# Gated attention block on one core: a batch's routing scratch moved into its PSUM bank, small normalisation steps moved or folded

## The reference

```python
x = x + tanh(g_xattn) * xattn(layernorm(x), ctx)      # windows of 128 columns, 8 heads of 32
x = x + tanh(g_ffn)   * ffn(layernorm(x))             # layernorm over the last axis, eps = 1e-5

def ffn(hidden):                                      # row of 2048 values per (batch, d)
    logits = flat @ router_weight.T + router_bias     # 64 experts
    scores = softmax(logits)
    topk_w, topk_idx = top_k(scores, 8)
    w_dense = scatter(topk_w, topk_idx)
    return flat * topk_w.sum() + w_dense @ expert_bias
```

## Time and profile before

| | us |
|---|---|
| median of 3 runs | 1213.76 |
| lowest, highest | 1210.02, 1215.45 |
| the profiled execution, its own time | 1211.18 |
| its span, first to last instruction | 1209.0 |
| mean granted clock of TensorE, share of full speed | 0.987 |

### The profile page before, as it was taken

How to read it: one execution, slowest core, us unless ns; L and a number is a source line. 1 busy time by engine, 2 the same in 40 slices (tenths; PEclk the granted TensorE clock), 3 DMA queues, 4 the chain that set the end, 5 groups by cost and what they waited for, 6 DMA issues and landing times.

```text
span 1209.0 us, 33323 instructions
## 1 busy us (share of the span) xinstructions
PE 1125.2 (93%) x11661; PEld 1045.5 (86%) x11661; DVE 975.0 (81%) x1882; ACT 1028.9 (85%) x3200; POOL 707.7 (59%) x660
## 2 busy tenths in 40 slices
PE   3699999999999899999999999998999999999977
PEld 3698999889988899798997989988998889979955
DVE  6667878988789877989779977988779987797757
ACT  4688999889989899988998989898898889989944
POOL 2365777467655567557764666646764656655621
PEclk9899999999999999999999999999999999999989
DMA  9267554785548854596546865478444884555433
GB/s 289 75 175 198 139 131 116 232 214 149 132 116 249 222 130 126 147 261 181 128 127 216 217 165 129 115 244 226 117 126 123 259 218 120 130 161 178 104 85 139
DMA packets 169766, 199.82 MB, mean 165 GB/s; under 512 B 27776, under 2 KB 104704, under 8 KB 169472
## 3 DMA queue, kind: packets, MB, share of 16 engines
q1 hardware_dynamic: 168736, 197.69, 60.3%
q10 hardware_dynamic: 864, 0.01, 0.0%
HBM read 80.06 MB, written 33.65 MB: 94 GB/s over the span
## 4 chain that ended last, share of the span: by engine, by line
PE 53%; SPq 21%; DVE 9%; ACT 5%; issue 5%; DMA 4%; POOL 3%; DVEq 0%; ACTq 0%; POOLq 0%
SPq L520 14%; PE ring L309 7%; PE ring L311 6%; PE ring L310 6%; PE ring L365 4%; DVE X L888 3%; PE ring L348 3%; PE ring L324 3%; PE ring L326 3%; PE ring L325 3%; PE ring L384 3%; PE ring L385 3%; PE ring L386 3%; SPq L525 3%; PE ring L403 3%
## 5 line engine op out<-in xcount | busy, mean ns | idle before, releaser
L614 ACT ACTIVATE P<-ring,nmx 128x128 f32<-128x128 f32 x1024 | 358.6, 403 | 32.1 <-DVE nmx L754 31.8
L309 PE MATMUL ring<-z_hi,wqk_hi 128*128 128x256 f32 x1024 | 299.3, 292 | 22.9 <-DVE z_lo L953 21.0
L310 PE MATMUL ring<-z_hi,wqk_lo 128*128 128x256 f32 x1024 | 292.3, 285 | 0.0
L311 PE MATMUL ring<-z_lo,wqk_hi 128*128 128x256 f32 x1024 | 292.2, 285 | 0.0
L614 ACT ACTIVATION_READ_ACCUMULATOR P<-ring,nmx 128x1 f32 x1024 | 248.9, 243 | 0.0
L1046 POOL TENSOR_TENSOR z_lo<-z,z_hi 128x1024 fp32r<-128x1024 f32 x62 | 147.6, 2381 | 166.8 <-ACT z_hi L582 166.8
L309 PEld LDWEIGHTS ring<-z_hi,wqk_hi 128*128 128x128 f32 x1024 | 198.0, 193 | 35.4 <-DVE wqk_lo L928 20.9
L1058 POOL TENSOR_TENSOR X<-X,xt 128x512 f32<-128x512 f32 x128 | 165.5, 1293 | 68.3 <-DVE xt L789 68.2
L761 DVE STREAM_TRANSPOSE T<-P 128x512 f32<-128x512 f32 x256 | 169.1, 690 | 44.6 <-ACT P L614 28.2
L311 PEld LDWEIGHTS ring<-z_lo,wqk_hi 128*128 128x128 f32 x1024 | 198.7, 194 | 0.0
L310 PEld LDWEIGHTS ring<-z_hi,wqk_lo 128*128 128x128 f32 x1024 | 198.5, 194 | 0.0
(11 more groups left out here) (137 smaller groups left out, 2696.1 us busy)
## 6 DMA issues: line engine op xcount, KB each, us to landing
PT<-T SPq DMA_DIRECT2D x1024, 80.0 KB, 2.1
cx<-in_ctx SPq DMA_DIRECT2D x128, 256.0 KB, 3.7
out_y<-X SPq DMA_DIRECT2D x128, 256.0 KB, 3.1
X<-in_x SPq DMA_DIRECT2D x112, 256.0 KB, 4.7
mg<-in_mask SPq DMA_DIRECT2D x64, 128.0 KB, 3.3
X<-in_x SPq DMA_DIRECT2D x8, 512.0 KB, 7.5
sel<-rows_d SPq DMA_DIRECT2D x256, 3.0 KB
X<-in_eb SPq DMA_DIRECT2D x2, 512.0 KB, 8.2
```

Source lines behind the costliest of these rows:

```text
L309: e.matmul(o, wqk_hi[:, t, cols], z_hi[:, t, :], t == 0, False)
L310: e.matmul(o, wqk_lo[:, t, cols], z_hi[:, t, :], False, False)
L311: last = e.matmul(o, wqk_hi[:, t, cols], z_lo[:, t, :], False, t == DT - 1)
L614: last = e.activation(P[:, n, :], bank("S", 4 * u + g)[:, k * W:(k + 1) * W], ACT.Exp, bias=nmx[u % 2][:, n:n + 1], accum_out=den[u % 2][: ...
```

## The change

- `lr` is gone. Its content is written into the unused half of the logits' own PSUM bank (`low(b)`); the product with the exponentials goes there too, and so do the sum of the weights and the gain in `c_scale`. That bank is now given back when `c_scale` is done (semaphore `ac_v`), at slot 40.75, and no longer at `c_top`'s (`lg_v`, slot 38.75).
- `c_gate` and `gate` are gone. `c_scale` makes the gain with one scalar_tensor_tensor and the bias with another, from `mv2` and `rs2`.
- The negated means are gone: the first normalisation subtracts the mean (`mv` is in two buffers for it), the second puts -1 in its formula.
- The eps additions leave VectorE; GpSimd adds eps, waits for itself, and raises to the power.

```diff
-            for b in batch(t, C["LT"]):
-                take(("LT", b), t, C["c_top"] - C["LT"], lg_v, b + 1)
+                take(("LT", b), t, C["c_sc"] - C["LT"], ac_v, b + 1)
...
             def norm2(b):                                  # VectorE
                 e.wait_ge(bn2_v, 16 * (b + 1))
+                if b:
+                    e.wait_ge(ac_v, b)
                 for t in range(DT):
                     e.bn_aggr(mv2[:, t, :], bn2[:, t, :, :].rearrange("p a c -> p (a c)")).then_inc(agg2_v, 1)
-                if b:
-                    e.wait_ge(ac_v, b)
-                e.wait_ge(agg2_v, DT * (b + 1))
-                e.tensor_scalar(ln2[:, 0, :], mv2[:, :, 0], -1.0, None, ALU.mult).then_inc(neg2_v, 1)
-                e.tensor_scalar(ln2[:, 1, :], mv2[:, :, 1], EPS, None, ALU.add).then_inc(neg2_v, 1)
...
-                e.wait_ge(rstd2_g, b + 1)
-                e.tensor_scalar(gate[:, 0, :], ln2[:, 2, :], cst[:, TF:TF + 1], None, ALU.mult).then_inc(dm_v, 1)
-                e.wait_ge(dm_v, b + 1)
-                e.tensor_tensor(gate[:, 1, :], gate[:, 0, :], ln2[:, 0, :], ALU.mult).then_inc(gate_v, 1)
...
-                    last = e.match_replace(lr[:, t, :], t8[:, t, :], lg[:, t, :], -3.0e38)
+                    last = e.match_replace(low(b)[:, t, :], t8[:, t, :], lg[:, t, :], -3.0e38)
                 last.then_inc(mr_v, 1)
                 e.wait_ge(mr_v, b + 1)
-                e.tensor_tensor(lr[:], lr[:], lg[:], ALU.not_equal).then_inc(sel_v, 1)
+                e.tensor_tensor(low(b), low(b), lg[:], ALU.not_equal).then_inc(sel_v, 1)
+
+            def low(b):
+                return bank("LT", b)[:, DT * NX:2 * DT * NX].rearrange("p (t x) -> p t x", t=DT)
...
-                e.tensor_tensor(ex[:], ex[:], lr[:], ALU.mult).then_inc(wm_v, 1)
+                e.tensor_tensor(low(b), low(b), ex[:], ALU.mult).then_inc(wm_v, 1)
...
-                e.tensor_reduce(sc[:, :, 5:6], w2[:, :, 0, :], AX.X, ALU.add).then_inc(wm_v, 1)
-                e.wait_ge(gate_v, b + 1)
+                wsum, gain = bank("LT", b)[:, 0:DT], bank("LT", b)[:, DT:2 * DT]
+                e.tensor_reduce(wsum, w2[:, :, 0, :], AX.X, ALU.add).then_inc(wm_v, 1)
                 e.wait_ge(wm_v, 4 * b + 3)
-                e.tensor_tensor(sc[:, :, 4:5], sc[:, :, 5:6], gate[:, 0, :].unsqueeze(2), ALU.mult).then_inc(wm_v, 1)
-                e.tensor_tensor(sc[:, :, 7:8], sc[:, :, 5:6], gate[:, 1, :].unsqueeze(2), ALU.mult)
+                e.scalar_tensor_tensor(out=gain, in0=wsum, scalar=cst[:, TF:TF + 1], in1=rs2[:], op0=ALU.mult,
+                                       op1=ALU.mult).then_inc(wm_v, 1)
                 e.wait_ge(wm_v, 4 * b + 4)
-                e.tensor_scalar(sc[:, :, 6:7], sc[:, :, 4:5], 1.0, None, ALU.add).then_inc(ac_v, 1)
+                e.scalar_tensor_tensor(out=sc[:, :, 7], in0=gain, scalar=-1.0, in1=mv2[:, :, 0], op0=ALU.mult, op1=ALU.mult)
+                e.tensor_scalar(sc[:, :, 6], gain, 1.0, None, ALU.add).then_inc(ac_v, 1)
...
             def norm2(b):                                  # GpSimd; input_norm in the same way
-                e.wait_ge(neg2_v, 2 * (b + 1))
-                e.tensor_tensor(ln2[:, 2, :], ln2[:, 1, :], half[:], ALU.pow).then_inc(rstd2_g, 1)
+                e.wait_ge(agg2_v, DT * (b + 1))
+                e.tensor_scalar(rs2[:], mv2[:, :, 1], EPS, None, ALU.add).then_inc(eps2_g, 1)
+                e.wait_ge(eps2_g, b + 1)
+                e.tensor_tensor(rs2[:], rs2[:], half[:], ALU.pow).then_inc(rstd2_g, 1)
```

More of the change, by code:

```diff
@@ L52 @@
     hT=37.5, hT_gap=0.25, ht_hi=41.25, ht_lo=41.75, R=47.25,
-    norm2=27.5, c_gate=33.5, L=36, LT=34, c_top=38.75, c_exp=37.75, c_w=40.75, c_sc=40.75, wT=43, wt_hi=43.25, wt_lo=42.25, mix=43.75, m_gap=0.25,
+    norm2=27.5, L=36, LT=34, c_top=38.75, c_exp=37.75, c_w=40.75, c_sc=40.75, wT=43, wt_hi=43.25, wt_lo=42.25, mix=43.75, m_gap=0.25,
     sx=44.75, sx_gap=1.25, x2=45.25, rl=48.5, rl_gap=2,
@@ L139, in gated_block_kernel @@
         bnst = sb("bnst", [128, DT, 4, 6])
-        mv = sb("mv", [128, DT, 2])
+        mv = [sb(f"mv{i}", [128, DT, 2]) for i in range(2)]
         bn2 = sb("bn2", [128, DT, 4, 6])
         mv2 = sb("mv2", [128, DT, 2])
-        ln1 = [sb(f"ln1_{i}", [128, 3, DT]) for i in range(2)]
-        ln2 = sb("ln2", [128, 3, DT])
+        rs1 = [sb(f"rs1_{i}", [128, DT]) for i in range(2)]
+        rs2 = sb("rs2", [128, DT])
         L = sb("L", [128, D])
@@ L195, in gated_block_kernel @@
         out_done = [[sem(f"out{t}{c}") for c in range(4)] for t in range(DT)]
-        bn1_v, agg1_v, neg1_v, rstd1_g = (sem(n) for n in ("bn1", "agg1", "neg1", "rstd1"))
+        bn1_v, agg1_v, eps1_g, rstd1_g = (sem(n) for n in ("bn1", "agg1", "eps1", "rstd1"))
         st_a = sem("st")
@@ L202, in gated_block_kernel @@
         gelu_a, othi_a, otlo_g, wo_pe, xt_v, x1_g = (sem(n) for n in ("gelu", "othi", "otlo", "WO", "xt", "x1"))
[L203 to L206, removed]
+        bn2_v, agg2_v, eps2_g, rstd2_g, ht_pe, hthi_a, htlo_v, r_pe = (sem(n) for n in (
+            "bn2", "agg2", "eps2", "rstd2", "hT", "hthi", "htlo", "R"))
+        l_a, lt_pe, lg_v, t8_v, neg_v, mr_v, sel_v, ex_a, w2_v, ac_v = (sem(n) for n in (
+            "L", "LT", "lg", "t8", "neg", "mr", "sel", "ex", "w2", "ac"))
         wm_v, wT_pe, wthi_a, wtlo_v, mix_pe, sx_a, x2_v = (sem(n) for n in (
@@ L835, in c_top @@
                     last = e.scalar_tensor_tensor(out=lg[:, t, :], in0=bank("LT", b)[:, t * NX:(t + 1) * NX],
-                                                  scalar=ln2[:, 2, t:t + 1], in1=rbb[:], op0=ALU.mult, op1=ALU.add)
+                                                  scalar=rs2[:, t:t + 1], in1=rbb[:], op0=ALU.mult, op1=ALU.add)
                 last.then_inc(lg_v, 1)
@@ L941, in _ @@
             input_norm(0)
-            ln = ln1[0]
             e.wait_ge(rstd1_g, 1)
@@ L945, in _ @@
                 for t in range(h.start, h.stop):
-                    last = e.tensor_scalar(z32[:, t, :], X[0][:, t, 0:U], ln[:, 0, t:t + 1], ln[:, 2, t:t + 1],
-                                           ALU.add, ALU.mult)
+                    last = e.tensor_scalar(z32[:, t, :], X[0][:, t, 0:U], mv[0][:, t, 0:1], rs1[0][:, t:t + 1],
+                                           ALU.subtract, ALU.mult)
                 last.then_inc(z32_g, 1)
@@ L1008, in _ @@
                         r_low(u, a)
-                for b in batch(t, C["c_gate"]):
-                    c_gate(b)
                 for b in batch(t, C["c_top"]):
@@ L1038, in z_full @@
                 for t in range(DT):
-                    last = e.tensor_scalar(z32[:, t, :], X[b % 2][:, t, c * U:(c + 1) * U], ln[:, 0, t:t + 1],
-                                           ln[:, 2, t:t + 1], ALU.add, ALU.mult)
+                    last = e.tensor_scalar(z32[:, t, :], X[b % 2][:, t, c * U:(c + 1) * U], mv[b % 2][:, t, 0:1],
+                                           rs1[b % 2][:, t:t + 1], ALU.subtract, ALU.mult)
                 last.then_inc(z32_g, 1)
```

32 lines of the change are left out of this document (11 added, 21 removed).

## The result

The changed kernel takes 1234.11 us (median of 4 runs, 1231.71 to 1236.63); the kernel before took 1211.89 beside it (1205.31 to 1215.45). The ratio is 1.0185, 95% interval 1.0153 to 1.0217: 1.9% slower. The forecast was 1211.4 in a range of 1206 to 1217, and none of the rivals gives this time. The profiled execution took 1235.34 us with a span of 1233.5.

A forecast was written before the change was run, and what follows sets the result against it. TensorE, busy 93% of the span, was taken as the bound, so only its waits count. Batch ends gain 2.5 us, PSUM writes lose 0.1: 1213.76 - 2.4 = 1211.4 us, range 1206 to 1217, no visible difference.

The forecast's parts named there:

- The failed step: First and second normalisation: dropping the negated means costs nothing either way, since mean and rstd enter the same instruction.
- the eps step: GpSimd before the power: the new eps instruction takes 0.2 us, bounded by 0.10 and 1.02; net effect taken as zero.
- The batch's end: Seven batch ends: the first add starts earlier, by 0.43 us in the third batch, 2.5 us in all.
- the first add released by the scaling: Batch's end on VectorE: the first add would wait for ScalarE's first scaling of x, no longer for the mix.
- ScalarE's eviction of v: Batch's end on ScalarE: it waits for TensorE's v, which nothing moves, so wt_hi behind it stays at 501.89.
- The new wait of v for divide: Batch's end on TensorE: v now waits for divide, at no cost with divide ending at 497.25, before 498.33.
- Writing and reading PSUM from VectorE: VectorE at batch ends: reading costs nothing visible; writing loses 0.1 us at the last batch's end, between 0 and 1.
- The rival of slow writes: Five VectorE writes into PSUM before divide: v is late once each costs 0.22 us more; 1223.5 us at 0.5; chance 0.10.
- the rival of stalls that stay: VectorE instructions with one PSUM operand still stall behind GpSimd, so only the gate goes: 1213.8 us; chance 0.10.
- The rival of SP's queue: SP's transpose DMAs start when divide is done and set the waits for PT: 7.0 us gained, 1206.8 us; chance 0.17.

The follow-up runs named there:

- the mended version: Changed kernel with the mean negated on VectorE into a small tile of its own and added on GpSimd: 1204.67 us, ratio 0.9927 to the kernel before.
- experiment 4: Third context buffer added to the changed kernel, slow subtract kept: 1209.52 us, ratio 0.9985; added to the version with the negated mean: 1203.98 us, ratio 0.9934.
- the scratch in SBUF: Version with the negated mean added, with low, wsum and gain back in SBUF and the logits' bank given back at lg: 1208.38 us, ratio 0.9977.
- the bare add: Changed kernel with one word changed, GpSimd's normalisation adding the mean instead of subtracting it, so the output differs: 1204.99 us, ratio 0.9926.

## Why the prediction was wrong

**The failed step** is the last sentence on eps: "The negated means cost nothing either way: mean and rstd enter the same instruction as before." The operands do; the operation was changed, and the price of an instruction was carried over from a row for (add, mult) to (subtract, mult) without a bound. The runs showed 1.24 us in place of 0.56, in each of 252 instructions, 171.4 us of GpSimd, and with it 0.0258 of the kernel's time, some 31 us. It should have been bounded like the eps step. The trace had no subtract with scalars on GpSimd. It had a subtract of two tensors (cx_lo, 1.28 us for 512 elements) beside an add of two tensors that takes as long; but that is another instruction, and its rows bound nothing here. A bound from above of twice the price, 252 times, would have made a slower case with a place and a price, if still a little short of the 2.2 times measured. No rival had one.

**The batch's end was mis-sized.** The mechanism was right: the gate gone, not_equal at 0.43 (told: 0.42), the three small products at 0.23, 0.17 and 0.15 (told: 0.2), the waits for ot_lo and wt_lo nearly gone, the first add released by the scaling:

```profile
513.25 1.28 DVE L880 TENSOR_TENSOR X<-X,ring 128x512 f32<-128x512 f32 x2 [1.22 <-ACT X L662]
```

The size was told as 0.43 us for the third batch. From TensorE's second group for v to the last score bank it went from 510.08 - 498.33 = 11.75 before to 518.36 - 508.07 = 10.29 now, 1.46 less; over the seven ends 81.8 became 71.5. First the two rows before the change, then the two after:

```profile
498.33 0.28 PE L324 MATMUL ring<-wv_hi,cx_hi 128*128 128x256 f32 x1
...
510.08 0.38 PE L340 MATMUL ring<-sel,ones 32*128 32x512 bf16 x1 [0.21 <-DVE X L888]
```
```profile
508.07 0.28 PE L322 MATMUL ring<-wv_hi,cx_hi 128*128 128x256 f32 x1
...
518.36 0.39 PE L338 MATMUL ring<-sel,ones 32*128 32x512 bf16 x1 [0.21 <-DVE X L880]
```

The step that failed in it reads "ScalarE's eviction of v at 499.96 waits for TensorE's v, which nothing moves". The timeline of ScalarE in the changed kernel:

```profile
508.14 0.63 ACT L629 ACTIVATE ot_hi<-o 128x512 fp32r<-128x512 f32 x1
508.67 0.37 ACT L602 ACTIVATE v<-ring 128x256 f32<-128x256 f32 x1
...
510.61 0.63 ACT L654 ACTIVATE wt_hi<-ring 128x512 fp32r<-128x512 f32 x1
511.08 2.13 ACT L662 ACTIVATE X<-X,sc 128x2048 f32<-128x2048 f32 x1
```

This eviction starts at 508.67, while TensorE's group for v, twelve matmuls of 0.12 from 508.07 on, runs until about 509.6. It evicts the v of the window before; the near fit in the earlier trace rows was chance. It stands behind ot_hi, which stands behind divide, so the whole list with wt_hi and the scaling moved with divide: counted from the second group for v, wt_hi starts at 2.54 us where it started at 3.56. These 1.02 and the 0.43 told make 1.45. Over the seven ends it is 10.3 us, against 2.5 told, and the mended version's gain (0.73%, 8.8 us) is about that.

**The two together**: the batch ends gave some 10 us in the trace, 0.0073 of the time (9 us) by the mended version, and the subtract took 0.0258 (31 us). The net is 0.0185, 22 us slower, where 2.4 us faster were told. Most of the 31 us came by a path that the prediction does not have: GpSimd's late cx_lo, SP's context load that waits for it, and the transpose DMAs queued behind (0.0200 of the 0.0258, experiment 4). Both steps failed, in opposite directions, and the larger gain of the batch ends hid over a quarter of what the subtract cost.

**What held.** The new wait of v for divide does not show. GpSimd's eps step takes 0.234 (told: 0.2), and the power behind it 1.04, so the 1.02 of before was the power's own price. Writing and reading PSUM from VectorE costs next to nothing: the masked product takes 405 ns in PSUM and 394 in SBUF, match_replace 218 and 209 (mended version, and with the scratch in SBUF), the sum of weights 428 and 422. The Trainium skill (Perfetto Trace Analysis, section Optimizing Scalar/DVE Operations) gives some 65 ns more of access overhead for a VectorE instruction on PSUM than for one on SBUF; these rows show 6 to 11, and here the measurement decides. The rival of slow writes is ruled out with its point at 0.22 us, and the rival of stalls that stay with not_equal at 0.43 and the second product at 0.17. The rival of SP's queue was right that the queue carries time to TensorE, but by another door: not through divide, through the context load that stands in front.

## What to carry to other kernels

When an edit changes an instruction's operation, price it as a new instruction, however equal its operands are, and if no row shows it, put wide bounds around the nearest one (here it was 2.2 times that). For an instruction that gets longer on an engine with idle time, follow the idle time: list what stands between it and each gap, who waits for each of those results, and what is queued behind that waiter. Before saying that a step waits for a producer, count which of the producer's results it takes.

## What the runs showed of the hardware

GpSimd's tensor-by-scalar instruction on 128 x 256 fp32 takes 0.56 us for an add and a multiplication in either order, 0.93 to 0.94 for one multiplication or for add with add, and 1.10 to 1.24 for all four forms tried with a subtract. On VectorE the same four instructions of the first unit take 1.38 us with the subtract as with the add. GpSimd's tensor-by-tensor subtract (1.30 us for 512 elements) and add (1.29) do not differ. Why the scalar form does stays open; the way round it, a negated operand made once per batch in an instruction of VectorE, costs nothing that is measured (ratio 0.9927 with it, 0.9926 with the bare add). TensorE's granted clock was 0.50 in a stretch that began some 2 us after an idle time of 1.93 us, and 0.950 in the mean of a run that had such a wait in nearly every unit (62 of 64), against 0.993 without them.
